# Relation sums of a four-layer graph network: an untransposed count table and whole counts, with the division moved behind the weight product

## The reference, cut to what matters

```python
seg = edge_type * n + dst
agg = segment_sum(x[src], seg, num_segments=N_REL * n)      # N_REL = 34, n = 256
cnt = segment_sum(ones, seg, num_segments=N_REL * n)
mean = agg.reshape(N_REL, n, -1) / jnp.maximum(cnt, 1.0).reshape(N_REL, n, 1)
h1 = jnp.einsum('rni,rio->no', mean, W_rel) + x @ W_root + b_rgcn
```

## Time and profile before

| | before |
|---|---|
| median of 3 runs | 1525.36 us (1523.99 to 1526.25) |
| the profiled execution, its own time | 1526.62 us |
| its span, first to last instruction | 1524.9 us |
| mean granted clock of TensorE | 0.936 of full speed |
| busy: PE, DVE, ACT, POOL | 1364.9, 1011.7, 655.7, 193.6 us |
| DMA | 229.45 MB, 150 GB/s over the span |

### The profile page before, as it was taken

The page is one execution under the profiler, slowest core; times in us unless marked ns, Lnnn a source line. Parts: engine busy times, 40 slices in busy tenths (PEclk is TensorE's granted clock), DMA queues, the critical chain, the costliest instruction groups (busy, mean ns, idle before and its releaser), DMA issues.

```text
span 1524.9 us, 22242 instructions
## 1 busy us (share of the span) xinstructions
PE 1364.9 (90%) x8269; PEld 1231.6 (81%) x8272; DVE 1011.7 (66%) x1669; ACT 655.7 (43%) x846; POOL 193.6 (13%) x134
## 2 busy tenths in 40 slices
PE   5699999866799999868688899999999999999886
PEld 4599999855799999758566799999999999999775
DVE  6889998867699998865545644555455554555444
ACT  1366655534466556524323334433343333433321
POOL 0024434302033223301000000000000000000000
PEclk9899999976799999979778999999999999999977
DMA  9456656544256666426132534344333443434500
GB/s 342 143 185 167 217 180 193 162 117 118 83 161 217 179 192 197 142 73 190 53 114 83 193 145 144 138 160 176 138 144 138 168 169 138 144 139 174 166 16 21
DMA packets 101300, 229.45 MB, mean 150 GB/s; under 512 B 8000, under 2 KB 34752, under 8 KB 101268
## 3 DMA queue, kind: packets, MB, share of 16 engines
q1 hardware_dynamic: 72780, 192.43, 35.9%
q10 hardware_dynamic: 19128, 28.08, 6.3%
q0 software_dynamic: 9360, 8.52, 3.9%
HBM read 210.27 MB, written 18.74 MB: 150 GB/s over the span
## 4 chain that ended last, share of the span: by engine, by line
PE 66%; DVE 19%; issue 6%; ACT 4%; another core or an unknown queue 2%; DMA 1%; DVEq 0%; ACTq 0%; SPq 0%
PE bank L375 64%; DVE w_lo L1055 4%; DVE hid_lo L1055 2%; DVE h_lo L1055 2%; ACT w_hi L793 2%; DVE neg_b L1198 1%; PE bank L712 1%; DVE scores_b L1143 1%; PE bank L409 1%; PE bank L476 1%; DVE scores_b L1145 1%; DVE same L1166 1%; DVE neg_b L1058 1%; DVE stats L1095 1%
## 5 line engine op out<-in xcount | busy, mean ns | idle before, releaser
L1055 DVE TENSOR_TENSOR w_lo<-w_in,w_hi 128x2304 fp32r<-128x2304 f32 (+5 forms) x160 | 390.9, 2475 | 91.7 <-ACT w_hi L793 91.6
L375 PE MATMUL bank<-w_hi,xT_hi 128*128 128x384 f32 (+3 forms) x942 | 329.8, 350 | 10.3 <-DVE w_lo L1055 6.2
L793 ACT ACTIVATE w_hi<-w_in 128x2304 fp32r<-128x2304 f32 (+5 forms) x160 | 323.8, 2061 | 23.2 <-PE bank L375 12.9
L375 PE MATMUL bank<-w_hi,hid_hi 128*128 128x512 f32 (+2 forms) x846 | 298.1, 352 | 22.5 <-DVE hid_lo L1055 21.1
L375 PE MATMUL bank<-w_lo,xT_hi 128*128 128x384 f32 (+3 forms) x942 | 312.0, 343 | 0.0
L375 PE MATMUL bank<-w_lo,hid_hi 128*128 128x512 f32 (+2 forms) x846 | 273.4, 343 | 0.0
L375 PE MATMUL bank<-w_hi,xT_lo 128*128 128x384 f32 (+3 forms) x942 | 249.5, 344 | 0.0
L375 PE MATMUL bank<-w_hi,hid_lo 128*128 128x512 f32 (+2 forms) x846 | 225.6, 344 | 0.0
L375 PEld LDWEIGHTS bank<-w_hi,hid_hi 128*128 128x128 f32 (+1 forms) x846 | 164.4, 194 | 58.1 <-DVE hid_lo L1055 20.0
L375 PEld LDWEIGHTS bank<-w_hi,xT_hi 128*128 128x128 f32 (+1 forms) x942 | 180.6, 192 | 37.4 <-issue 6.9
L375 PEld LDWEIGHTS bank<-w_lo,xT_hi 128*128 128x128 f32 (+1 forms) x942 | 180.6, 192 | 14.0 <-issue 0.8
(11 more groups left out here) (207 smaller groups left out, 1549.2 us busy)
## 6 DMA issues: line engine op xcount, KB each, us to landing
w_in<-L_gnn_W_rel SPq DMA_DIRECT2D x68, 1152.0 KB, 5.7
w_in<-L_gnn_W SPq DMA_DIRECT2D x66, 1152.0 KB, 5.9
table<-zrow SPq DMA_DIRECT2D x1, 9216.0 KB, 34.9
scores_b<-table ACTq DMA_DIRECT2D x36, 256.0 KB, 2.6
a_bc<-L_gnn_a_src ACTq DMA_DIRECT2D x18, 384.0 KB, 3.8
a_bc<-L_gnn_a_dst ACTq DMA_DIRECT2D x18, 384.0 KB, 5.0
w_in<-ffn_out SPq DMA_DIRECT2D x4, 864.0 KB, 7.4
w_in<-L_ffn_W SPq DMA_DIRECT2D x3, 1152.0 KB, 5.7
```

Source lines behind the costliest of these rows:

```text
L375: return pe.matmul(out, lhsT, rhs, start=start, stop=stop, **kw)
L793: act.activation(out, ps, func, **kw).then_inc(mark, 1)
L1055: return dve.tensor_tensor(out, a, b, op)
```

## The change

The table becomes a table of cells: one row for each (type, source), one column for each destination, and each edge adds to one cell. PE and ACT no longer make rows. DVE builds the key of a cell, PE transposes all 64 columns of keys once, ACT writes them to DRAM, and SP loads 512 keys to all partitions for each batch (`load_key`, 256 KB). `first` becomes the number of equal keys in the batch, by a product with a triangle of 1 and 257; edges that are not the first go to a spill cell. POOL still issues 4 indirect adds for a batch, now of 128 single floats each, and one more small operation.

In the relation stage the counts are read untransposed and used whole as the moving operand (whole numbers up to 4096 have no low part), so `mean` has 24 matmuls instead of 36, `turn_rel` and `aT` are gone, and DVE's `shares` becomes one minimum with 4096 (`counts`). The division by the degree is moved behind the weight product: each relation's product is closed in its own banks (0, 2 for tile 0; 1, 6 for tile 1), and DVE adds it to the sum `xn` scaled by 1/degree (`accumulate`, two instructions for a tile). The degrees by type come from the first count: its source one-hots get 34 more columns (290 instead of 256), in two banks.

What counts above 4096 leave over is handled by a 35th round: nine small DVE operations in layer 1's feed-forward find the relation that has such counts, one small matmul spreads its number, POOL gathers its weights (6 indirect DMAs of 128 rows of 3 KB) and its counts (2 of 128 rows of 1 KB), and PE runs one mean of 24 matmuls of 128 columns and one product of 36, which DVE adds for both tiles. The chunks behind it (GCN, last feed-forward) move one place, so their halves are exchanged.

The core of the diff:

```diff
-DUMP = REL * N
-ROWS = DUMP + 2 * N
+DUMP = REL * N * N
+ROWS = REL * N + 2 * N
+DUPLICATE = 256.0
+EXACT = 4096.0
...
+            def load_key(b):
+                sp.wait_ge(b_same, b)
+                sp.dma_start(flat(key_row[:, :, :]), key_rows[bass.ds(b, 1), :].rearrange("a n -> (a n)").partition_broadcast(P)).then_inc(ld_key, 16)
...
-                pool.wait_ge(b_kept, b * 2 + (g // 2 + 1))
                 pool.wait_ge(e_added, b * (16 * G) + (16 * g + 16))
                 pool.indirect_dma_start(
-                    out=table, out_offset=bass.IndirectOffsetOnAxis(ap=row_i[:, g:g + 1], axis=0),
-                    in_=rows[:, g, :], in_offset=None, compute_op=ALU.add).then_inc(e_added, 16)
+                    out=cells, out_offset=bass.IndirectOffsetOnAxis(ap=row_i[:, g:g + 1], axis=0),
+                    in_=value[:, g:g + 1], in_offset=None, compute_op=ALU.add).then_inc(e_added, 16)
...
+            pool.wait_ge(x_rows, 1)
+            n = nth(C_REL + REL)
+            for p in range(2):
+                pool.wait_ge(w_high[p], n)
+                pool.wait_ge(w_low[p], n)
+                for k in range(3):
+                    pool.indirect_dma_start(out=w_in[:, p, k, :], ... in_=t["L3_gnn_W_rel"], ...).then_inc(w_gathered[p], 16)
+                if p == 0:
+                    pool.wait_ge(e_added, 16 * ET + 16)
+                    pool.wait_ge(r_count, REL - 1)
+                    for m in range(M):
+                        pool.indirect_dma_start(out=ct[:, 0, m, :], ... in_=table, ...).then_inc(ld_excess, 16)
...
                 with pe.Fori(1, HEADS) as h:
-                    batch_keys(h + (b0 - 1))
                     up(h, h * 2 + n0)          # its batch_rows are gone too
...
-            seed((0, 1, 2))
+            def product(m, lhs, half, mark=None, before=0):
+                for k in range(K):
+                    last = mm3([(bank[b][:, c0:c1], of_w(half)(k, o, o + c1 - c0)) for (b, c0, c1, o) in REL_BANKS[m]],
+                               lhs[k], k == 0, k == K - 1)
+                return last
-            def mean(r):
-                pe.wait_ge(r_tlow, r + 1)
+            def mean(r, half):
+                pe.wait_ge(r_count, r + 1)
...
-                            last = mm3([(bank[3 + j][:, (k % 2) * N:(k % 2 + 1) * N], part(aT_hi, aT_lo, slice(0, P), sm))],
-                                       of_h(sm, k * P, (k + 1) * P), sm == 0, sm == M - 1)
+                            for b, h in enumerate(of_h(sm, k * P, (k + 1) * P)):
+                                last = mm(bank[3 + j][:, (k % 2) * N:(k % 2 + 1) * N], h, REL_C[half][:, sm, :],
+                                          sm + b == 0, sm + b == 2)
...
+            def relation(r, half, following):
+                pe.wait_ge(r_low, r * 3 + 3)
+                weights(r + nth(C_REL))
+                pe.wait_ge(r_acc, r * 2 + 1)
+                product(0, node_tile(*REL_T[half], 0, K), half).then_inc(r_out, 1)
+                following()
+                pe.wait_ge(r_acc, r * 2 + 2)
+                product(1, node_tile(*REL_T[half], 1, K), half).then_inc(w_used, 1)
...
+            relation(REL - 1, 1, excess)
+            pe.wait_ge(r_low, REL * 3 + 3)
+            weights(REL + nth(C_REL))
+            pe.wait_ge(r_acc, REL * 2 + 1)
+            product(0, node_tile(*REL_T[0], 0, K), 0).then_inc(w_used, 1)
...
+            def round_means(r, half, more):
+                if more:
+                    act.wait_ge(r_count, r + 1)
+                    load_counts(r + 2, half)
+                high(r + nth(C_REL), r + used(C_REL - 2), half)
+                for j in range(3):
+                    act.wait_ge(r_mm, r * 3 + (j + 1))
+                    keep(flat(REL_T[half][0][:, 2 * j:2 * j + 2, :]), bank[3 + j][:, :], r_high)
...
             def batch_firsts(b):
-                dve.wait_ge(b_key, b + 1)
+                dve.wait_ge(ld_key, b * 16 + 16)
...
-                tt(kdiag[:, :, :], same[:, :, :], tril[:, :].unsqueeze(1).to_broadcast([P, G, P]), mul).then_inc(b_tri, 1)
-                dve.tensor_reduce(first[:, :], kdiag[:, :, :], AX.X, mx).then_inc(b_first, 1)
+                for g in range(G):
+                    last = dot(same_w[:, g, :], same[:, g, :], tril[:, :], first[:, g:g + 1])
+                step(last)
+                ts(again[:, :], first[:, :], DUPLICATE, ALU.is_ge).then_inc(b_first, 1)
...
             def one_hot(b, a):
+                tt(all_src[:, a, :, N:N + REL], iota[:, 0:REL].unsqueeze(1).to_broadcast([P, G, REL]),
+                   edge_f[:, 2, bass.ds(b * G, G)].unsqueeze(2).to_broadcast([P, G, REL]), ALU.is_equal)
...
+            def counts(half, landed):
+                dve.wait_ge(ld_ct[half], landed)
+                ts(flat(REL_C[half][:, :, :]), flat(ct[:, half, :, :]), EXACT, ALU.min).then_inc(r_count, 1)
+            def weighted(m, banks, weight):
+                for (b, c0, c1, o) in banks:
+                    xs = xn[:, m, o:o + c1 - c0]
+                    last = dve.scalar_tensor_tensor(xs, bank[b][:, c0:c1], weight, xs, mul, add_)
+                return last
+            def accumulate(r, m):
+                summed(r + 1, m)
+                weighted(m, REL_BANKS[m], rinv[:, m, bass.ds(r, 1)]).then_inc(r_acc, 1)
...
+            with dve.Fori(1, REL // 2) as i:
+                for half in range(2):
+                    r = i * 2 + half
+                    counts(half, i * 16 + 16)
+                    dve.wait_ge(r_acc, r * 2 - 1)
+                    accumulate(r - 2, 1)
+                    low(r + nth(C_REL), half)
+                    accumulate(r - 1, 0)
+                    mean_low(r, half)
```

More of the change, by code:

```diff
@@ L348, in batch @@
                     add(b, g)
[L350 to L355, removed]
-                with step.loop(1, HEADS - 1, 3) as h:
-                    head(h)
-                batch(HEADS - 2 + b0)
-                batch(HEADS - 1 + b0)
             pool.wait_ge(consts, NCONST)
@@ L723, in mean, with excess @@
                     last.then_inc(r_mm, 1)
[L725 to L727 removed]
+            def excess():
+                pe.wait_ge(r_count, REL + 1)
+                for j in range(3):
+                    for k in (2 * j, 2 * j + 1):
+                        for sm in range(M):
+                            for b, h in enumerate(of_h(sm, k * P, (k + 1) * P)):
+                                last = mm(bank[3 + j][:, (k % 2) * P:(k % 2 + 1) * P], h, REL_C[0][:, sm, 0:P],
+                                          sm + b == 0, sm + b == 2)
+                    last.then_inc(r_mm, 1)
@@ L795, in _, with high @@
             odd_rows = [0, 0]
-            def high(n, free, half, shape=WHOLE, parts=(0, 1)):
+            def high(n, free, half, shape=WHOLE, parts=(0, 1), loaded=None):
                 rows_, tiles, cols = shape
@@ new lines, in _ @@
+            counts(0, 16)
+            low(nth(C_REL), 0)
+            mean_low(0, 0)
+            counts(1, 16)
+            for m in range(M):
+                root(m)
+                dve.wait_ge(r_acc, m + 1)
+            low(nth(C_REL) + 1, 1)
+            accumulate(0, 0)
+            mean_low(1, 1)
+            with dve.Fori(1, REL // 2) as i:
+                for half in range(2):
+                    r = i * 2 + half
[5 more added lines that the diff above has]
+                    mean_low(r, half)
@@ L1467, in _ @@
+            excess(16 * M)
+            dve.wait_ge(r_acc, REL * 2 - 1)
+            accumulate(REL - 2, 1)
+            low(nth(C_REL) + REL, 0)
+            accumulate(REL - 1, 0)
+            for j in range(3):
+                dve.wait_ge(r_high, REL * 3 + (j + 1))
+                low_of(REL_T[0][1][:, 2 * j:2 * j + 2, 0:P], bank[3 + j][:, 0:N].rearrange("p (k n) -> p k n", k=2),
+                       REL_T[0][0][:, 2 * j:2 * j + 2, 0:P], r_low)
+            accumulate(REL - 1, 1)
             low_chunk(C_GCN3)
-            dve.wait_ge(w_used, used(C_REL + REL - 1))
+            dve.wait_ge(r_acc, REL * 2 + 2)
@@ L1469, in _ @@
+            dve.wait_ge(w_used, used(C_REL + REL))
             for m in range(M):
-                for (b, c0, c1, o) in SUM_BANKS[m]:
-                    last = tt(xn[:, m, o:o + c1 - c0], bank[b][:, c0:c1], hbias_bc[:, o:o + c1 - c0], add_)
-                last.then_inc(ln_xn, 1)
+                weighted(m, REL_BANKS[0], xinv[:, m:m + 1]).then_inc(ln_xn, 1)
             transposed(7)
```

258 lines of the change are left out of this document (139 added, 119 removed).

## The result

| | median of the runs, us | runs |
|---|---|---|
| before | 1525.8 (1523.99 to 1527.6) | 4 |
| after | 1471.28 (1469.09 to 1472.76) | 4 |
| after, once more, beside other runs of before | 1470.46 (1468.63 to 1473.66) | 4 |

The ratio of after to before is 0.9641, 95% interval 0.9625 to 0.9658: 54.5 us or 3.6% faster. The forecast was 1469, with a range of 1455 to 1486. The profiled execution took 1471.03 us, its span is 1469.0 (before 1524.9).

A forecast was written before the change was run, and what follows sets the result against it. PE bounds the relation stage, busy 570 of 570 us; DVE's chain matters in the heads. Relation stage 52.7 + heads 7.4 - count 3.8 = 56.3 us off 1526.6 gives 1470.3, as median 1469; forecast 1461 to 1478, range 1455 to 1486.

The forecast's parts named there:

- The relation round: Relation stage: without 12 mean matmuls and the transposes, PE's round falls from 17.28 to 15.41 us, with 4 us slack.
- The rival of the loads: Relation rounds: weight loads taking 11.9 us would set a round of 16.5 us, 1506 us in all; chance 0.05.
- The start: Start of relations: two gaps and the seeds go; round 1 begins at 855.2 against 864.1, with 1.4 us for lower clock.
- The end: End of relations: excess round, gathers and GCN weights put `ln_xn` at 1378.5 against 1431.15; stage gain 52.7 us.
- The two additions of 2 us: End of relations: 2 us for POOL's slower issue and 2 for the lower clock, added to 1374.5.
- The heads: Attention heads: `batch_firsts` takes 2.0 us instead of 2.49, in 7 heads of each layer, 7.4 us gained.
- The rival of 11 us more: Attention heads: they fall to PE's own length, 11 us more gain, 1458 us; chance 0.08.
- The count: Count at the front: a 136-column operation in each of 16 batches and a second key operation lose 3.8 us, bounds 2 and 5.
- The extra copies: Count at the front: five extra copies of counts lie beside the load of `a_bc` and cost nothing.
- The stages between: Outside heads, count and relations: small operations fall into idle time and cost nothing; without the cover 2.5 us.
- GpSimd: Heads: POOL's adds become the path if slower than 7.9 us each; chance 0.05, whole gain lost in half of it.
- The prediction's 1537 for an add of 9.5 us: Heads: if POOL's cell adds took 9.5 us each, the kernel would end at 1537 us, slower than before.

The follow-up runs named there:

- The undone pass: Kernel after, with 12 further matmuls of 256 columns in each of the 34 means, results unread: 1519.18 us, ratio 0.9945.
- the experiment: Kernel after, with two further indirect adds of zeros per batch into neighbouring spare cells on GpSimd: 1600.87 us, ratio 1.0464.

## Why the prediction was right, point by point

**The relation round** was the main term and held: 15.52 us against 15.41, PE without a gap, 4.8 us of slack where the text had 4. The term was small by 0.10 a round: the products take 6.32 and not 6.29, and a mean's matmul 0.120 and not 0.118. That is 3.3 us over 32 rounds. The undone pass prices 12 matmuls at 1.41 us, as the prediction did. By the formula that the prediction took from the Trainium skill (TensorE: Matmul & The Clock Gate, Back-to-back issue gap) they would be 1.31. That section gives it for a matmul by itself, and says that in a stream in which each matmul has its weight load both set the spacing; the prediction left this out. The trace does not agree with the formula: 24 of them take 2.88 us, 0.120 each.

The rival of the loads did not come: the 68 loads of relation weights took 5.5 us in median, and PE waited for nothing in the rounds.

**The start** was forecast for a root product of 13.6 us; it took 15.05 (816.62 to 831.67), because PE began it at a granted clock of 0.50 for 5 us, where the kernel before was granted 0.78. That is the 1.4 us by which the row of product 0 misses its forecast. In the new kernel the wait after the first mean is 2.67 us, the 3 of the text, and the lower clock behind it cost 1.6 us, for which 1.4 was set.

```profile
816.60:821.70 5.10, 5.08 (x16) 4.33 (x17) 4.90 (x6) 1.42 (x2) 0.00 (x0) 0.50 0.31 103
```

```profile
819.00:824.00 5.00, 4.96 (x22) 4.00 (x22) 4.97 (x6) 1.95 (x3) 0.00 (x0) 0.78 0.32 105
```

The first window is of after, the second of before.

**The end** was 5.4 us shorter than forecast: product 0 of round 33 to `ln_xn` took 24.8 us, not 30.2. The two additions of 2 us, for GpSimd's slower issues and for the lower clock, fell away: the first of the eight issues took 2.46 us and the others 0.95 to 0.97. ACT still waited 2.86 us for the second part of the gathered weights, but its low part was ready at 1360.9, before PE asked for it at 1366.26, so PE never waited for them.

```profile
1350.36 0.95 POOL L396 DMA_INDIRECT w_in<-L_gnn_W_rel,xrow_i  x1 [0.30 <-issue]
1351.61 0.95 POOL L396 DMA_INDIRECT w_in<-L_gnn_W_rel,xrow_i  x1 [0.30 <-issue]
...
1356.20 2.13 ACT L831 ACTIVATE w_hi<-w_in 128x2304 fp32r<-128x2304 f32 x1 [2.86 <-DMA w_in<-L_gnn_W_rel,xrow_i]
```

The excess mean took 2.63 us, 0.11 a matmul of 128 columns, near the 2.8 chosen between 2.2 and 5.5. As foreseen the GCN weights' low parts (until 1373.57) come last ahead of the weighted sums, 1 us behind product 34. The errors of the rounds and of the end nearly cancel: the stage won 53.0 us, 52.7 were forecast. That the sum is so close is luck.

**The heads** won 7.3 us, 7.4 were forecast: `batch_firsts` takes 1.95 us (176.70 to 178.65), the text had 2.0. Its own terms give a little less than it wrote, 14 x (2.49 - 2.0) = 6.9. That VectorE is the path was shown by moving this work, and that PE's own length lies some 0.9 us a head lower. The rival of 11 us more was thus a real bound, but it needs another order of VectorE's work, and then 9 us can be followed to it.

**The count** cost 3.0 us, 3.8 were forecast, within its bounds. Each comparison costs 0.21 us, near the 0.22 assumed, 3.4 us in all; the step that was missing is that the kernel before waited 2.0 us for PE's buffers among its one-hots, and the new work took that place. The extra copies, costed at nothing, then take some of it back: the first head lost 3.0 though the last one-hot lost only 1.9.

**The stages between** were costed at nothing and gave back 1.8 us: 0.9 between the layers, 0.9 between the last head and the root. Of the second part the clock is a visible share. Around the end of layer 2's GCN the window of after has clock 0.67, that of before 0.86:

```profile
745.00:770.00 25.00, 17.36 (x74) 15.17 (x73) 12.47 (x20) 8.13 (x13) 0.00 (x0) 0.67 0.09 21
```

```profile
745.00:770.00 25.00, 17.27 (x89) 14.65 (x87) 10.62 (x20) 10.12 (x17) 0.00 (x0) 0.86 0.16 56
```

The transposes there take 2.82 us and took 1.94. Why the clock falls in one and not in the other is open, as is the first 0.9 us. Between the variants of this kernel such stages differ by up to 3 us with the same instructions, so a forecast that is right to less than that is right by luck.

**GpSimd** did not become the path: its last add lies near 661 us and was at 711. Its batches begin 29 to 35 us apart, 31.4 in the mean of layer 0's first seven, as the heads do, and no row of VectorE's waits names GpSimd, so the lead of one batch is not used up; the experiment shows what it takes. (The prediction's 1537 for an add of 9.5 us does not follow from its own rule, which gives 6 x (43 - 31.4) - 30 = 40 us a layer, 1548; nothing else hangs on it.) For the rule of the Trainium skill that below 512 bytes a DMA does a read-modify-write (DMA: Bandwidth & Descriptors, Specifications) the case shows no cost by size: the kernel's own cell adds land in 5.2 us, where rows of 1 KB took 5.5. Whether the slow neighbouring cells have to do with that rule, no run shows.

## What to carry to other kernels

Where PE is busy without a gap, count its matmuls; an engine beside it costs nothing until its chain from product to product is as long, and that length can be read off one round and then held to. Look at what a new operation displaces: here a wait for a buffer hid half of the price, and gaps of 1 us ahead of ELU could hold all of the work that set the heads' length. Where a scatter sends many unwanted elements to a dump at once, spread the dump; it was tried here with whole adds of 128, while the kernel itself sends only the edges there that meet another of their cell in a batch.

## What was not expected of the hardware

- An indirect add of one float for each of 128 partitions landed in 8.9 us when the 128 cells were neighbours, in 4.0 when they lay 1 KB apart, and rows of 1 KB in 4.6. Over 32 such adds the kernels differ by 112 us (1600.87 and 1489.17), VectorE's waits for them included.
- PE waited 2.67 us ahead of product 0 of round 0 and was granted 0.60 from 838 to 842 us; after a wait of 1.70 us at the same place it was granted 1.00. A wait shorter by 1.0 us gave 2.5 us back, 1.6 of them by the clock.
- GpSimd issued an indirect DMA in 0.95 us at the end of the relations, where in the heads one took between 1.55 and 3.9 us (median 1.59).
